# Tile 0's first two steps ahead of tile 1's coefficients, tile 1's convolution ahead of its Sobel, its divergence behind steps, and two passes on ScalarE

## The reference, cut to what matters

```python
g  = relu(_bn(_dwconv(h, wg),  ...))
g1 = relu(_bn(_dwconv(h, wg1), ...))
gy, gx = _sobel(h)
Dx = 1.0 / (gy * gy / LAM2 + 1.0);  Dy = 1.0 / (gx * gx / LAM2 + 1.0)
ux = 0.5 * (roll(g, 1, axis=2) - roll(g, -1, axis=2))
vy = 0.5 * (roll(g1, 1, axis=3) - roll(g1, -1, axis=3))
Ax, Ay, Bx, By, E = g * DT, g1 * DT, Dx * DT, Dy * DT, (ux + vy) * DT
D = 1.0 / (1.0 + 2.0 * Bx + 2.0 * By)
cm_x, cp_x = (-Ax + 2.0 * Bx, Ax + 2.0 * Bx)
cm_y, cp_y = (-Ay + 2.0 * By, Ay + 2.0 * By)
c0 = 1.0 - 2.0 * Bx - 2.0 * By
for _ in range(5):
    prev = h
    h = D * (c0 * h0 - 2.0 * E * h + cm_x * roll(h, 1, axis=2) + cp_x * roll(h, -1, axis=2)
             + cm_y * roll(h, 1, axis=3) + cp_y * roll(h, -1, axis=3))
    h = h + D * (2.0 * DT) * fsrc
    h0 = prev
x = x + relu(_bn(h, ...))
x = x + relu(conv3x3(_gn(x), alpha * ternary(W)) + b)
```

## Time and profile before

| What | Value |
|---|---|
| median of three runs | 278.0 us |
| profiled execution, its own time | 277.91 us |
| its span in the trace | 276.1 us |
| VectorE (DVE) busy | 247.2 us, 90% of the span |
| TensorE (PE) busy | 233.6 us, 85% |
| ScalarE (ACT) busy | 133.8 us, 48% |
| Pool busy | 16.8 us, 6% |

### The profile page before, as it was taken

One profiled execution on the slowest core, in us unless ns is written; L12 is line 12 of the kernel. 1 busy time (PEld: TensorE's weight loads), 2 busy tenths in 40 slices (PEclk: granted clock), 3 DMA queues, 4 the chain that ended last, 5 costly groups with the idle time before them and its releaser, 6 DMA issues.

```text
span 276.1 us, 5235 instructions
## 1 busy us (share of the span) xinstructions
PE 233.6 (85%) x2276; PEld 209.6 (76%) x2276; DVE 247.2 (90%) x196; ACT 133.8 (48%) x207; POOL 16.8 (6%) x36
## 2 busy tenths in 40 slices
PE   0137999999959999279999999999999987889793
PEld 0136889989925588279989999898989986767683
DVE  3799999999999989999998999999999989886821
ACT  3294776879860054702623425160603246917743
POOL 2000000003310201101000101010101000000000
PEclk9999999999979999959999999999999999999999
DMA  6950000005998771990700334248610030000124
GB/s 213 350 116 0 0 4 6 2 0 112 199 205 253 152 152 38 209 209 2 154 0 2 76 78 94 61 116 190 129 26 1 0 138 17 2 0 0 62 93 152
DMA packets 7190, 24.94 MB, mean 90 GB/s; under 512 B 2816, under 2 KB 3328, under 8 KB 5120
## 3 DMA queue, kind: packets, MB, share of 16 engines
q0 software_dynamic: 2304, 14.68, 26.6%
q1 hardware_dynamic: 4720, 9.61, 10.6%
q10 hardware_dynamic: 144, 0.33, 0.4%
HBM read 6.79 MB, written 2.10 MB: 32 GB/s over the span
## 4 chain that ended last, share of the span: by engine, by line
DVE 54%; PE 27%; issue 9%; ACT 7%; DMA 1%; DVEq 0%; ACTq 0%
DVE ring L918 24%; DVE coef L653 8%; PE psum L1180 8%; PE psum L1170 6%; ACT coef L380 5%; PE psum L1257 5%; DVE first_two L1004 4%; PE psum L1117 3%; PE psum L1087 3%; DVE state L729 2%; DVE coef L964 1%; DMA bn<-in_norms 1%; DVE ring L722 1%; DVE hi_s L734 1%; DVE gsum L687 1%
## 5 line engine op out<-in xcount | busy, mean ns | idle before, releaser
L918 DVE TENSOR_TENSOR ring<-coef,state 128x2048 f32<-128x2048 f32 x51 | 113.5, 2286 | 2.1 <-PE psum L1180 1.9
L1180 PE MATMUL psum<-mats,ring 128*128 128x128 f32 x816 | 96.6, 278 | 9.6 <-DVE ring L918 9.5
L1180 PEld LDWEIGHTS psum<-mats,ring 128*128 128x128 f32 x816 | 91.4, 144 | 13.3 <-DVE ring L918 12.9
L380 ACT ACTIVATE state<-psum 128x1024 f32<-128x1024 f32 x36 | 35.1, 1028 | 74.3 <-PE psum L1180 60.2
L653 DVE SCALAR_TENSOR_TENSOR coef<-coef 128x2048 f32<-128x2048 f32 x16 | 36.4, 2290 | 0.7 <-issue 0.2
L380 ACT ACTIVATE coef<-coef 128x2048 f32<-128x2048 f32 (+1 forms) x10 | 17.6, 1783 | 10.1 <-DMA coef<-coef 9.9
L1257 PE MATMUL psum<-hi,dense_m 128*128 128x512 f32 (+1 forms) x54 | 20.0, 379 | 0.9 <-ACT coef L380 0.9
L1139 PEld LDWEIGHTS psum<-coef,state 32*128 32x128 f32 x672 | 19.4, 187 | 1.4 <-issue 1.3
L380 ACT ACTIVATE coef<-psum 128x512 f32<-128x512 f32 (+2 forms) x23 | 17.5, 766 | 5.4 <-PE psum L1117 4.3
L1139 PE MATMUL psum<-coef,state 32*128 32x64 f32 x672 | 20.0, 271 | 0.0
L1257 PE MATMUL psum<-lo,dense_m 128*128 128x512 f32 (+1 forms) x54 | 19.5, 369 | 0.0
(11 more groups left out here) (133 smaller groups left out, 280.4 us busy)
## 6 DMA issues: line engine op xcount, KB each, us to landing
first_two<-coef POOLq DMA_DIRECT2D x7, 1024.0 KB, 8.5
coef<-coef POOLq DMA_DIRECT2D x5, 1024.0 KB, 8.8
coef<-in_x SPq DMA_DIRECT2D x2, 1024.0 KB, 6.0
coef<-in_wide_taps SPq DMA_DIRECT2D x3, 384.0 KB, 7.6
ring<-in_x SPq DMA_DIRECT2D x2, 512.0 KB, 6.0
ring<-in_x SPq DMA_DIRECT2D x1, 1024.0 KB, 10.3
coef<-coef SPq DMA_DIRECT2D x1, 1024.0 KB, 7.6
out<-coef SPq DMA_DIRECT2D x2, 512.0 KB, 3.1
```

Of the source, the lines that this page charges most:

```text
L380: return nc.scalar.activation(dst, src, func, **kw)
L918: V.tensor_tensor(wc(ring[:, slot, :]), wc(coef[:, t, a, :]), h_at(t, k, dw, dc), ALU.mult)\
L1180: ins = mm(slot_ap(name)[:, (j % 8) * 128:(j % 8) * 128 + 128], src[:, j * 128:j * 128 + 128], ident, is_transpose=True, start=first and j ...
```

## The change

The diff changes the order of the programs and some homes of data:

- PE's jobs are put in another order, with other slots: tile 0's high parts of gy ahead of its low parts, var_1 behind gy, alpha between gx_0_0 and gx_0_1, tile 1's depthwise convolution ahead of its Sobel sums, dv_1_0 behind back_to_natural of (0,0) and dv_1_1 behind the products of (1,0).
- VectorE makes over_channels(0), source(0) and step (0,0) ahead of newton(1), with divergence_added, denominator(1) and ask_out between the products; then newton(1), out_norm, across_rows(1), across_columns(1), step (1,0), and only then over_rows(1), over_channels(1), divergence_taken and source(1). Step (0,0) adds its source on PE behind product 3 (before: behind product 2).
- Two passes go to ScalarE: the grouped s of tile 1 (reorder instead of scale_grouped(1)) and the high part of tile 0 (split_hi(0)).
- Tile 1 gets its own parts for the Sobel sums (s_parts1, in planes 3 and 4 of its coefficients), and tile 0's source another home (source_at[0]). The sum of tile 0's diffusivities, D and the first pass of over_rows(0) are cut in halves. In the first steps the ring is used in falling order. d_of(1), a0_of(1) and copy_s(1) move into ScalarE's loop over the steps. In the end the second rsqrt of ScalarE comes ahead of relu_dense(0, 0).

Its core, cut (coef[:, t, ...] becomes coef[t][:, ...] throughout):

```diff
     early = [("mean_0", 0), ("var_0", 1), ("mean_1", 2), ("wsum", 0), ("t2_0_0", 3), ("t2_0_1", 0), ("gy_0_0", 1),
...
+             ("gy_0_1", 2), ("var_1", 0), ("gx_0_0", 3), ("alpha", 1), ("gx_0_1", 0), ("cv_0_0", 2), ("cv_0_1", 3),
+             ("cv_0_2", 0), ("cv_0_3", 1), ("t2_1_0", 2), ("t2_1_1", 3), ("cv_1_0", 0), ("cv_1_1", 2), ("cv_1_2", 1),
+             ("cv_1_3", 3), ("gy_1_0", 0), ("gy_1_1", 2), ("gx_1_0", 1), ("gx_1_1", 3)]
...
+            def split_hi(t):
+
+                act.wait_ge(s_ready, t + 1)
+                copy(wc(s_parts[t][0][:, :]), h_at(t, 0)).then_inc(s_hi, 1)
...
+            def reorder(t):
+
+                act.wait_ge(s_ready, t + 1)
+                copy(s_grouped[t].rearrange("p (g a w e) -> p a w g e", e=2, a=CP, w=W),
+                     h_at(t, 0).rearrange("p w (a g e) -> p a w g e", a=CP, e=2)).then_inc(s_grouped_ready, 1)
...
-            scale_taps(range(5, 8))
+            scale_taps(range(5, 13))
+            split_hi(0)
+            square_of(1)
             to_depthwise(0, 0)
             to_depthwise(0, 1)
...
             sobel_square(0, 0, 0)
             sobel_square(0, 0, 1)
+            rsqrt_first(128, GROUPS)
+            scale_taps(range(13, 16))
             sobel_square(0, 1, 0)
...
             sobel_square(0, 1, 1)
...
+            reorder(1)
+            wrap(0, 0, s_halo)
             reciprocal_first(0)
...
                 keep_turned(k, t, 0)
                 keep_turned(k, t, 1)
+                if (k, t) == ORDER[1]:
+                    act.wait_ge(ayp_ready, 2)
+                    wait_job(act, "dv_1_1")
+                    copy_s(1)
...
                 wrap(t, k + 1, halo_ready)
                 if (k, t) == ORDER[0]:
...
                     source_of(0)
-                if (k, t) == ORDER[1]:
+                    d_of(1)
+                    a0_of(1)
+                if (k, t) == ORDER[2]:
                     source_of(1)
...
             relu_bn_out(1, 1)
+            rsqrt_first(128, BT)
             relu_dense(0, 0)
-            rsqrt_first(128, BT)
...
-            ternary()
+            ternary_count()
             ask_scale(1)
+            ternary_kept()
+            rsqrt(128, GROUPS, root(1), wide=True)
+            scale_s(1)
+            weight_scale()
             ternary_sign()
-            rsqrt(128, GROUPS, root(1), wide=True)
-            scale_grouped(1)
             shifted(0)
             denominator(0)
-            scale_s(1)
             split_hi(1)
             split_lo(1)
             newton(0)
             across_columns(0)
+            channel_difference()
             across_rows(0)
             both_diffusivities(0)
-            channel_difference()
             over_rows(0)
...
-            denominator(1)
             over_channels(0)
+            source(0)
+            step(0, 0, ((1, divergence_added), (2, lambda: denominator(1)), (3, ask_out)))
             newton(1)
+            out_norm()
             across_rows(1)
             across_columns(1)
...
-            step(0, 0)
+            step(1, 0)
             over_rows(1)
             over_channels(1)
             divergence_taken()
             source(1)
-            step(1, 0)
             for k, t in ORDER[2:-1]:
...
-            sobel(0, 0, 0)
-            sobel(0, 0, 1)
+            for n in range(2):
+                sobel(0, 0, 0, (n,))
+                sobel(0, 0, 1, (n,))
+            group_var(1)
             sobel(0, 1, 0)
-            group_var(1)
+            pe.wait_ge(kept_ready, 1)
+            small("alpha", 2, ones[:, :], wred[:, 3:5])
             sobel(0, 1, 1)
...
             for k, t in ORDER:
...
+                if last is not None and last[0] < STEPS - 1 and last[1] == t:
+                    back_to_natural(*last)
+                if (k, t) == ORDER[1]:
+                    divergence(0)
+                if (k, t) == ORDER[2]:
+                    divergence(1)
                     back_to_natural(*last)
                 if (k, t) == ORDER[-1]:
                     group_mean2(0)
                 take_sums(t, k)
+                if k == 0:
+                    add_products(t, k, ((3, lambda: add_source(t, 0, False)),), True)
+                    last = (k, t)
+                    continue
                 add_source(t, k)
```

More of the change, by code:

```diff
@@ L326, in first_source @@
                 pool.wait_ge(s_copied[t], 1)
-                pool.dma_start(first_two[t][:, :], coef[:, t, FS, :], accum_op=ALU.add).then_inc(first_full[t], 16)
+                pool.dma_start(first_two[t][:, :], source_at[t], accum_op=ALU.add).then_inc(first_full[t], 16)
             pool.wait_ge(e_made, 3)
@@ L424, in sobel_square @@
                 wait_job(act, name)
-                frees(copy(half(coef[:, t, g, :], h), slot_ap(name), ACT.Square, scale=0.5 * S ** 0.5), name)
+                frees(copy(half(coef[t][:, g, :], h), slot_ap(name), ACT.Square, scale=0.5 * S ** 0.5), name)
             def to_natural(t, q):
@@ L537, in relu_bn_out @@
                 wait_job(act, name)
-                frees(copy(half(coef[:, t, 0, :], h), slot_ap(name), ACT.Relu, scale=outw[:, 2:3],
+                frees(copy(half(coef[t][:, 0, :], h), slot_ap(name), ACT.Relu, scale=outw[:, 2:3],
                            bias=outw[:, 3:4]), name)
@@ L572, in take_out @@
                 wait_job(act, name)
[L573 removed]
+                frees(copy(part(coef[t][:, 4, :], t, h), part_slot(name, t, h)), name)
             def keep_turned(k, t, h):
@@ L777, in _, with ternary_count @@
             scale_s(0)
-            split_hi(0)
+            centre(1)
             split_lo(0)
-            centre(1)
             sum_squares(1)
-            def ternary():
+            def ternary_count():
                 dve.wait_ge(vsum_ready, 4)
@@ L837, in both_diffusivities @@
                 dve.wait_ge(column_part, t + 1)
-                signal(V.tensor_tensor(coef[:, t, 2, :], coef[:, t, 4, :], coef[:, t, 5, :], ALU.add), sb_ready, t + 1)
+                for h in range(2):
+                    V.tensor_tensor(half(coef[t][:, 2, :], h), half(coef[t][:, 4, :], h), half(coef[t][:, 5, :], h), ALU.add)\
+                        .then_inc(sb_ready, 1)
             def taken_out(t):
@@ L847, in over_rows @@
                 taken_out(t)
-                dve.wait_ge(d_ready, t + 1)
                 dve.wait_ge(row_part, t + 1)
                 dve.wait_ge(column_part, t + 1)
-                then(stt(coef[:, t, AXM, :], gN[t], 2.0, coef[:, t, 0, :], ALU.mult, ALU.mult))
-                stt(coef[:, t, AXP, :], coef[:, t, AXM, :], -0.5, coef[:, t, AXP, :], ALU.mult, ALU.add)\
+                if t:
+                    dve.wait_ge(d_ready, 3)
+                    then(stt(coef[t][:, AXM, :], gN[t], 2.0, coef[t][:, 0, :], ALU.mult, ALU.mult))
+                else:
+                    for h in range(2):
+                        dve.wait_ge(d_ready, h + 1)
+                        done = mark(stt(half(coef[t][:, AXM, :], h), half(gN[t], h), 2.0, half(coef[t][:, 0, :], h),
+                                        ALU.mult, ALU.mult))
+                    done()
+                stt(coef[t][:, AXP, :], coef[t][:, AXM, :], -0.5, coef[t][:, AXP, :], ALU.mult, ALU.add)\
                     .then_inc(axp_ready, 1)
@@ L1118, in sobel @@
                                      sobel_m[:, m, :], part[:, frm * C:(frm + count) * C],
-                                     start=(i == 0 and part is s_parts[0]), stop=(i == last and part is s_parts[1]),
+                                     start=(i == 0 and n == 0), stop=(i == last and n == 1),
                                      skip_group_check=True)
-                ins.then_inc(pe_job, 1)
+                if passes[-1] == 1:
+                    ins.then_inc(pe_job, 1)
             def depthwise(t, h):
@@ L1210, in add_products @@
                     pe.wait_ge(product, summed[0] + 1)
-                    ins = add_turned(t, k, ring[:, summed[0] % RING, :], first and i == 0, i == count - 1)
+                    ins = add_turned(t, k, ring[:, -summed[0] % RING, :], first and i == 0, i == count - 1)
                     summed[0] += 1
```

225 lines of the change are left out of this document (112 added, 113 removed), and 3 rows, old and new, of the table early.

## The result

| | before | after |
|---|---|---|
| median of four runs each | 278.4 us | 306.75 us |
| ratio of the two | | 1.101 (1.097 to 1.106) |
| profiled execution, its own time | 277.91 us | 307.07 us |
| span | 276.1 us | 305.3 us |
| VectorE busy | 247.2 us | 244.2 us |

The change makes the kernel 28.4 us slower; +27.4 was forecast. VectorE has 3 us less to do, so it is all waits. Three rows of the page of the changed kernel: the groups of products, of the copies of state, and of the transposes of first_two. In each the last part is the idle time of the engine just before them and what ended most of it.

What follows compares the result with a forecast made beforehand. VectorE was taken as the bound, with Pool's and SP's DMA queues deciding the new waits. −0.4 + 24.5 + 2.9 + 1.5 − 1.1 = +27.4 us on 277.9 gave 305.3 us, range 300 to 311.

Steps and rivals of the forecast that it cites:

- The long wait: VectorE idle from 102.5 to 127.0 ahead of step (1,0), tile 0's source queued behind tile 1's sum on Pool: +24.5 us.
- the low clock: PE at the 1.2 GHz level after 26 us idle, for the source and some of the product: 1.4 us added.
- VectorE up to across_columns(1): VectorE's new order up to the end of tile 1's columns: ends at 102.5 against 102.9, −0.4 us.
- the wait for var(1): VectorE, early: var(1) at 34.2, VectorE ready at 33.05, a wait of 1.1 instead of 0.4, +0.8 us.
- e_full: Step (0,0), divergence_added between the products: both pieces of e0 landed at 79.8 to 80.9, 80.4 taken, +2.2 us.
- the sum for cut passes and pairs: VectorE's ledger up to the end of tile 1's columns: +0.9 us for cut passes and dependent pairs.
- Behind the wait: VectorE after step (1,0) starts: +2.9 us at its fourth product, +1.5 at the wait at 148.23, −1.1 at the end.
- the tail: End of the kernel: ScalarE's second rsqrt ahead of relu_dense(0,0), its share of normalise(1) starts 1.1 us earlier: −1.1 us.
- quick transfers: Rival, SP's copy and Pool's adds: transfers quick when alone, first_full(0) at 113.65, 4.1 sooner: 301.2; chance 0.06.
- That the source can pass the wait: Rival, Pool's queue: L327 isn't held by the wait ahead of L340, no 24.5 or 2.9: 277.9 or 275.7; chance 0.06.
- A clock that stays low under divergence(0): Rival, PE after 26 us idle: divergence(0) at 1.2 GHz takes twice 7.8 us, +7.8, 313; chance 0.04.
- The cover: ScalarE's reorder(1) ends at about 41.6, its reader on PE starts no sooner than 50.4; double cost still hidden.

Runs made afterwards that it cites:

- source_first: The changed kernel with first_source(0) ahead of the waits for sb_begun and column_part in Pool's program: 279.49 us, 1.0043 times the kernel before.
- columns_late: The kernel before with across_rows(1) and across_columns(1) behind step (0,0) on VectorE: 296.31 us, 1.063 times the kernel before.
- norm_late: The changed kernel with out_norm behind across_rows(1) and across_columns(1) instead of ahead of them: 304.58 us, 2.2 under the changed kernel.
- divergence_in_wait: The changed kernel with divergence(0) on PE between product 3 and the source of step (0,0), instead of behind back_to_natural(0,0): 303.36 us.
- norm_first_before: The kernel before with ScalarE's second rsqrt ahead of relu_dense(0,0): 277.26 us, 0.9956 times the kernel before.
- reorder_before: The kernel before with ScalarE's reorder(1) in place of scale_grouped(1), and scale_s(1) ahead of shifted(0): 286.94 us, 1.031 times the kernel before.

## Why the prediction was right, point by point

- **The long wait.** 25.02 us were measured, +24.5 forecast, at the place, with the releaser and by the mechanism that were named. source_first shows the mechanism by taking it away; columns_late brings about the late source once more (PE idles 20.25 us for it), though there most of VectorE's wait is for the sum. The steps that were named came as well: u of tile 0 at 44.9, product 0 at 74.4, Pool's add at 106.11, step (0,1) at 158.2.
- **Its terms.** across_rows(1) ended at 101.2 (forecast 100.3). SP's copy took 4.6 us (5.2 taken). L350 to first_full(0): 106.11 to 118.06, 11.95 us (11.9). From the start of the source at 118.11 to back_to_natural 6.47 us (5.4). To step (1,0) 3.87 (3.85). The one that was off is PE: 1.4 us were added for the low clock, and it is 2.5. I had taken the level to last for about 3.5 us of work; it lasted beyond the source's 3.5 us into the product (2.67 for a product that takes 1.8). That the 25.02 come so near the 24.5 is in part luck: the 1.1 us that PE took longer stand against a copy that was 0.6 us quicker than taken.
- **VectorE up to across_columns(1).** It ended at 103.4, 0.5 behind the kernel before, where 0.4 ahead was forecast. The step that failed is the wait for var(1): 1.1 us forecast, 2.48 in this execution. Sobel 0's first products were priced at the durations of before, although PE has a gap of 0.9 us ahead of them now; norm_late's 0.55 us shows that it need not come so. e_full came at 81.5 and not 80.4 (+0.6), and the sum for cut passes and pairs (0.9) was too high and hid a part of both.
- **Behind the wait.** 2.71 us in step (1,0) (2.9 forecast, shown by divergence_in_wait); 2.67 instead of 0.69 in step (2,0), +2.0 (1.5 forecast, not tried alone; the forecast took PE's clock as full there, but PE idles 6.28 us ahead of step (0,1), its granted clock is 0.50 from 160 to 164, and in norm_late, where the same 64 transposes took 10.03 us instead of 8.86, VectorE's waits from step (0,1) to (2,0) add up to 3.35 us); the tail −1.2 (−1.1, shown by norm_first_before).
- **The sum.** +0.5 + 25.0 + 2.7 + 2.0 − 1.2 = 29.0, for 29.2 between the two spans. The medians are 28.4 apart, as the profiled execution of the changed kernel lies 0.3 over its median and that of the kernel before 0.5 under its own. Without the two waits that go with the queue, the same terms give +1.3, and source_first measured +1.2. One slip in the chances: the rival of the quick transfers stood at 301.2, inside 300 to 311, so about 0.10 lay outside and not 0.15.
- **The rivals.** That the source can pass the wait: no, 0.54 us behind L350. Quick transfers: the copy was, 4.6 us, and the estimate by the Trainium skill's rule (DMA: Bandwidth & Descriptors, anatomy of one DMA on the SWDGE path, which is the path of Pool's DMAs; this copy is SP's) was 4.4; the two adds were not, 11.95 us with nothing else on the engines (197 GB/s from 108 to 110), so there the trace doesn't agree. A clock that stays low under divergence(0): no, it was at 0.72 from 122 to 124 and at 1.00 from 124.
- **The cover.** reorder(1) was said to be hidden and was, in the changed kernel (it ended at 42.5, its reader came at 52.4). In the kernel before the same pass was hidden as well, and yet it cost 8 us by what it let VectorE, and so Pool, do earlier. Such a thing had no place in the prediction: PE of the changed kernel has a gap of 1.0 us at 68.44 and the low clock from there to about 75, and it did no harm because the Sobel sums of tile 1 were wanted just as they came: shifted(1) ended at 86.0, VectorE asked for it at 86.2.

## What to carry to other kernels

Before a step is moved ahead of another, read the queues of all engines that wait for either: an engine which hands over DMAs one by one holds back everything behind its next wait, and an order that costs nothing while all its waits end early costs the full length of the chain once one of them ends late. Moving the one line that is wanted first is then worth more than all passes that were taken off the bound engine. Work taken off that engine pays only up to its next wait, so look for that wait, and for what else will start earlier, before counting it.

## What the runs showed of the hardware that was not expected

- **PE stood still, by all signs for want of instructions, behind data.** The gap of 2.75 us came when the one packet of the queue "instruction" moved at 69 to 70 instead of 65 to 66, behind 1 MB of Pool's accumulating DMA, and went when this DMA was held for 1.6 us. By the Trainium skill (Runtime: NRT & Kernel Launch, section on instruction fetch mechanics), each engine fetches its next block of instructions by a DMA queue of its own while it runs the block before, and the cost is mostly hidden; reorder_before shows a case where it isn't, 2.75 us and what follows. That the packet was PE's isn't shown by a row; it is argued from the nine gaps that all end 2.2 to 2.5 us behind such a packet.
- **What follows costs more than the gap.** After 2.75 us of standing still the granted clock was at the 1.2 GHz level from 72 to 92, although PE had work in most of this time; after 25 us of idling in the changed kernel it was back at 1.00 within 6 us. The convolution of tile 1 ended 8.8 us later than in the kernel before (84.85 against 76.07), 2.75 of it the gap; the rest is put down to the clock. Why it stayed low so long is open.
- **The same matmuls, 5.15 or 3.21 us.** In the four traces read where PE has a gap of 0.9 us ahead of Sobel 0, with the program the same up to there, these 14 matmuls took 5.15, 5.35, 3.21 and 3.20 us. The order of the kernel before, with gaps of 0.22 to 0.55 us, shows less of it: the first 7 of them took 1.71 to 2.54 us.
